# Selecting experts sequence by sequence, and modulating the token rows on GpSimd, in a two-layer adaLN kernel

## The reference

```python
h = _layernorm(x) * (1 + cb) + sb              # the modulated tokens
scores = sigmoid(h @ w_router); sfc = scores + corr_bias       # 32 columns
group_scores = sum of the 2 best sfc of each of 8 groups of 4
masked = sfc where the group is one of the 4 best, else -inf
topk_idx = top_k(masked, 6);  topk_w = scores at topk_idx
routed = sum over the 6 experts of topk_w * (silu(h @ gate_w) * (h @ up_w)) @ down_w
shared = (silu(h @ sh_gate_w) * (h @ sh_up_w)) @ sh_down_w
x = x + gb * (routed + shared)
```

## Time and profile before

| | us |
|---|---|
| median of 3 runs | 491.87 (491.0 to 492.24) |
| profiled execution | 492.93 |
| its span | 491.1 |
| PE busy | 411.1 (84%) |
| DVE busy | 310.0 (63%) |
| ACT busy | 191.6 (39%) |
| POOL busy | 130.9 (27%) |

### The profile page before, as it was taken

The page is one execution under the profiler, slowest core; times in us unless marked ns, Lnnn a source line. Parts: engine busy times, 40 slices in busy tenths (PEclk is TensorE's granted clock), DMA queues, the critical chain, the costliest instruction groups (busy, mean ns, idle before and its releaser), DMA issues. The chain is left out here.

```text
span 491.1 us, 5936 instructions
## 1 busy us (share of the span) xinstructions
PE 411.1 (84%) x1819; PEld 293.8 (60%) x1820; DVE 310.0 (63%) x726; ACT 191.6 (39%) x332; POOL 130.9 (27%) x143
## 2 busy tenths in 40 slices
PE   2888524598699999999998797389898999799995
PEld 0342123454477777777776536267676778688885
DVE  3489996879434444444443479868677956865432
ACT  2168670323222222222222144272696169422430
POOL 0160000000367777777777302000000000000000
PEclk9999775769799999999999989599999799899998
DMA  8309867395122333333337287700400000000101
GB/s 280 138 20 356 317 173 197 111 390 237 42 86 98 101 102 107 95 103 102 106 106 254 83 296 273 232 5 17 177 0 1 1 0 1 0 0 10 35 1 43
DMA packets 22878, 57.64 MB, mean 117 GB/s; under 512 B 3267, under 2 KB 14021, under 8 KB 21865
## 3 DMA queue, kind: packets, MB, share of 16 engines
q1 hardware_dynamic: 17432, 42.57, 25.4%
q0 software_dynamic: 5424, 14.82, 9.5%
HBM read 46.87 MB, written 10.51 MB: 117 GB/s over the span
## 5 line engine op out<-in xcount | busy, mean ns | idle before, releaser
L642 PE MATMUL bank<-arena,tile_mem 128*128 x224 | 76.8, 466 | 0.0
L1173 POOL DMA_INDIRECT tile_mem<-h_dram,gidx x57 | 55.4, 972 | 54.1 <-DVE gidx L1521 36.7
L1143 POOL TENSOR_TENSOR rstd<-ve,mhalf 128x4 f32<-128x4 f32 x8 | 8.1, 1015 | 212.6 <-DVE ve L1273 212.6
L1537 DVE TENSOR_TENSOR tile_mem<-tile_mem,bank 128x176 f32<-128x176 f32 x56 | 19.0, 338 | 68.7 <-ACT tile_mem L987 68.7
L1180 POOL DMA_INDIRECT y_dram<-norm,didx x56 | 55.3, 988 | 24.6 <-issue 13.4
L658 PE MATMUL bank<-arena,tile_mem 88*128 x224 | 57.7, 379 | 0.8 <-DVE tile_mem L1532 0.8
L658 PEld LDWEIGHTS bank<-arena,tile_mem 88*128 88x128 f32 x224 | 42.4, 190 | 15.8 <-issue 1.0
L738 PE MATMUL bank<-x_r,f_r 128*128 128x512 f32 x192 | 46.8, 404 | 4.3 <-DVE arena L1712 3.2
L642 PEld LDWEIGHTS bank<-arena,tile_mem 128*128 128x128 f32 x224 | 38.7, 193 | 12.1 <-issue 0.5
L738 PEld LDWEIGHTS bank<-x_r,f_r 128*128 128x128 f32 x192 | 36.6, 193 | 13.4 <-DVE arena L1712 3.7
L982 ACT ACTIVATE tile_mem<-bank 128x256 f32<-128x256 f32 x57 | 21.9, 384 | 51.4 <-PE bank L635 50.5
(11 more groups left out here) (244 smaller groups left out, 708.9 us busy)
## 6 DMA issues: line engine op xcount, KB each, us to landing
arena<-w_gu SPq DMA_DIRECT2D x3, 2112.0 KB, 14.0
arena<-y_dram SPq DMA_DIRECT2D x8, 768.0 KB, 5.8
arena<-w_dn SPq DMA_DIRECT2D x4, 1408.0 KB
arena<-w_gu SPq DMA_DIRECT2D x2, 2464.0 KB, 16.4
arena<-w_f SPq DMA_DIRECT2D x6, 512.0 KB, 7.5
arena<-w_conv SPq DMA_DIRECT2D x5, 320.0 KB, 5.8
arena<-wmod SPq DMA_DIRECT2D x3, 512.0 KB, 8.4
arena<-wmod SPq DMA_DIRECT2D x2, 768.0 KB, 6.7
```

The costliest lines, as they stand in the source:

```text
L642: mm = pe.matmul(bank[2 + r % 2][:, 0:2 * M], xgT[r % 2][:, k * P:(k + 1) * P], gu[:, bass.ds(e[k], 2 * M)], start=(k == 0), stop=(k == CT ...
L1173: pool.indirect_dma_start(out=xg[j % 4], out_offset=None, in_=h2_dram, in_offset=bass.IndirectOffsetOnAxis(ap=gidx[:, j:j + 1].bitcast(U32 ...
L1537: tt(hid[r % 2], sil[r % 2], bank[2 + r % 2][:, M:2 * M], ALU.mult).then_inc(hid_ready, 1)
```

## The change

The selection is put into a function `choose(b)` that handles the four tiles of one sequence. ScalarE takes the sigmoid of sequence 0 right after the modulation of sequence 0, and that of sequence 1 after the modulation of sequence 1; `logit_done`, `score_ready` and `mask_ready` count the sequences. TensorE waits for the scores of sequence 0 before it writes the logits of sequence 1 to the same bank. The four modulating operations move from VectorE to GpSimd (`unmix`), behind its four inverse roots. Shift and scale rows and the temporaries get other places in memory (the temporaries in the one-hot memory, in `cmp8` and in `pos`). ScalarE's wait for the modulated rows ahead of the shared expert goes.

```diff
--- before.py
+++ after.py
@@ -47,6 +47,7 @@
 SHM = 2 * M
 SHT = 3
 SH_ROWS = [P, P, SHM - 2 * P]
+TOPS = NT * (3 * G + 2 * (G + 8 - TOPG) + 8)
 SLOT_TILES = 80
 QUADS = SLOT_TILES // 4
 TAIL = 3
@@ -168,27 +169,13 @@
         hidT = [tile_mem[0:MH, o + i * 2 * P:o + (i + 1) * 2 * P] for i in range(2)]; o += 2 * C
         yt = [norm[:, TB + r, :] for r in range(4)]
         modrow0 = tile_mem[0:B, 0:6 * C]
-        modB0 = tile_mem[:, 6 * C:6 * C + B * 3 * C].rearrange("p (b n) -> p b n", b=B)
+        ga0 = tile_mem[:, 6 * C:6 * C + B * C].rearrange("p (b n) -> p b n", b=B)
+        h2_rows = tile_mem[:, (SHT + 1) * S:(SHT + 1) * S + B * 2 * C].rearrange("p (b n) -> p b n", b=B)
         sh_hid = tile_mem[:, 0:SHT * S].rearrange("p (m n) -> p m n", m=SHT)
         sh_sil = tile_mem[:, SHT * S:(SHT + 1) * S]
 
 
         scores = sb("scores", [P, NT, E])
-        o = (SHT + 1) * S
-
-        def temp(*shape):
-            nonlocal o
-            n = NT * int(np.prod(shape))
-            o += n
-            assert o <= TW
-            names = "abc"[:len(shape)]
-            return tile_mem[:, o - n:o].rearrange(f"p (t {' '.join(names)}) -> p t {' '.join(names)}",
-                                                  t=NT, **dict(zip(names, shape)))
-        sfc = temp(E)
-        hi2, lo2 = temp(G, 2), temp(G, 2)
-        m1, m2, m3 = temp(G), temp(G), temp(G)
-        gsx, gtop, grep = temp(G + 8 - TOPG), temp(8), temp(G + 8 - TOPG)
-        gmask, gpen = temp(G), temp(G)
         sfx = sb("sfx", [P, NT, E + 8 - TOPK])
         stop8 = sb("stop8", [P, NT, 8])
         srep = sb("srep", [P, NT, E + 8 - TOPK])
@@ -198,6 +185,7 @@
         ones16 = sb("ones16", [P, P], BF16)
         iota16 = sb("iota16", [P, P], F16)
         cmp8 = sb("cmp8", [P, E, G])
+        assert E * G == 2 * NT * G * 2
         ntile = sb("ntile", [P, E])
         incl = sb("incl", [P, E])
         onesE = sb("onesE", [P, E])
@@ -210,10 +198,27 @@
         wk = sb("wk", [P, NT, TOPK])
         OS = 8
         onehot_s = sb("onehot_s", [P, OS, P], F16)
+        assert 2 * TOPS <= OS * P
 
         OJ = TB * TOPK
         onehot_j = nc.alloc_sbuf_tensor_at("onehot_j", [P, OJ, SLOT_TILES + 1], F16, offset=norm_at + 4 * TB * C)
         assert OJ * (SLOT_TILES + 1) <= 2 * TB * C
+
+
+        tops_mem = onehot_s[:, :, :].rearrange("p o q -> p (o q)").bitcast(F32)[:, 0:TOPS]
+        sfc = pos[:, :, :]
+        hi2, lo2 = [cmp8[:, 16 * i:16 * (i + 1), :].rearrange("p e g -> p (e g)").rearrange("p (t g a) -> p t g a", t=NT, a=2)
+                    for i in range(2)]
+        o = 0
+
+        def temp(n):
+            nonlocal o
+            o += NT * n
+            assert o <= TOPS
+            return tops_mem[:, o - NT * n:o].rearrange("p (t a) -> p t a", t=NT)
+        m1, m2, m3 = temp(G), temp(G), temp(G)
+        gsx, gtop, grep = temp(G + 8 - TOPG), temp(8), temp(G + 8 - TOPG)
+        gmask, gpen = m1, m2
         ejcmp = sb("ejcmp", [SLOT_TILES, E])
         ej = sb("ej", [SLOT_TILES, 1])
         eoff = sb("eoff", [1, SLOT_TILES + 8], I32)
@@ -402,8 +407,8 @@
             sp_.dma_start(modg_dram, modg[0:B, :]).then_inc(mod_out[0], 16)
             sp_.wait_ge(mod_out[0], 32)
             for b in range(B):
-                for dst, row, at in ((modB0[:, b, 0:C], modg_dram, 0), (modB0[:, b, C:2 * C], mod_dram[0], SB),
-                                     (modB0[:, b, 2 * C:3 * C], modg_dram, 2), (gb0[:, b, :], modg_dram, 1)):
+                for dst, row, at in ((ga0[:, b, :], modg_dram, 0), (h2_rows[:, b, 0:C], mod_dram[0], SB),
+                                     (h2_rows[:, b, C:2 * C], modg_dram, 2), (gb0[:, b, :], modg_dram, 1)):
                     src = row[b:b + 1, at * C:(at + 1) * C].to_broadcast([P, C])
                     sp_.dma_start(dst, src).then_inc(modB_in[0], 16)
 
@@ -565,11 +570,13 @@
                 transposes(B + b, b, (x_done, b + 1))
 
                 pe.wait_ge(hT_ready, CT * (B + b + 1))
+                if b:
+                    pe.wait_ge(score_ready, b)
                 for t in range(b * TB, (b + 1) * TB):
                     for k in range(CT):
                         mm = pe.matmul(bank[6][:, t * E:(t + 1) * E], hT[:, k, t * P:(t + 1) * P], router[:, k, :],
                                        start=(k == 0), stop=(k == CT - 1))
-            mm.then_inc(logit_done, 1)
+                mm.then_inc(logit_done, 1)
 
 
             def shared_in(b, parts):
@@ -596,7 +603,7 @@
             pe.wait_ge(modcol_ready, 3)
             shared_in(0, range(3))
 
-            pe.wait_ge(mask_ready, 1)
+            pe.wait_ge(mask_ready, B)
             m16 = mask16[:, :, :].rearrange("p t e -> p (t e)")
             pe.matmul(bank[0][:, 0:NT * E], tri16[:, :], m16, start=True, stop=False, skip_group_check=True)
             for d in range(1, NT):
@@ -605,7 +612,7 @@
             for t in range(NT):
                 mm = pe.matmul(bank[1][:, 0:E], ones16[:, :], m16[:, t * E:(t + 1) * E], start=(t == 0), stop=(t == NT - 1))
             mm.then_inc(rank_done, 1)
-            pe.wait_ge(score_ready, 1)
+            pe.wait_ge(score_ready, B)
             shared_in(0, range(3, 2 * SHT))
 
             pe.wait_ge(ej_ready, 1)
@@ -942,10 +949,16 @@
                 ins = act.activation(dst[:, w * sc:w * (sc + 1)], bank[4][:, w * sc:w * (sc + 1)], ACT.Identity, bias=1.0)
             ins.then_inc(modcol_ready, 1)
             modulated(2, 0, 0, SB, CB)
+
+            def token_scores(b):
+
+                act.wait_ge(logit_done, b + 1)
+                act.activation(scores[:, b * TB:(b + 1) * TB, :].rearrange("p t e -> p (t e)"),
+                               bank[6][:, b * TB * E:(b + 1) * TB * E], ACT.Sigmoid).then_inc(score_ready, 1)
+
+            token_scores(0)
             modulated(3, 1, 0, SB, CB)
-            act.wait_ge(logit_done, 1)
-            act.activation(scores[:, :, :].rearrange("p t e -> p (t e)"), bank[6][:, 0:NT * E], ACT.Sigmoid)\
-               .then_inc(score_ready, 1)
+            token_scores(1)
 
             def shared_silu(b, extra=None):
                 for m in range(SHT):
@@ -967,7 +980,6 @@
                     ins = act.activation(dst, bank[banks[h]][:, :], ACT.Copy)
                 ins.then_inc(shy_ready, 1)
 
-            act.wait_ge(h2_ready, B)
             shared_silu(0)
 
             for t in range(NT):
@@ -1166,6 +1178,20 @@
             for n in range(B, 2 * B):
                 inverse_root(n)
 
+            def unmix(b):
+
+                pool.wait_ge(normT_done, CT * (B + b + 1))
+                pool.wait_ge(norm_ready, B + b + 1)
+                v = norm[:, b * TB:(b + 1) * TB, :]
+                sh, sc = [h2_rows[:, b, i * C:(i + 1) * C].unsqueeze(1).to_broadcast([P, TB, C]) for i in range(2)]
+                step(pool.tensor_tensor(v, v, sc, ALU.mult))
+                settle()
+                pool.tensor_tensor(v, v, sh, ALU.add).then_inc(h2_ready, 1)
+
+            pool.wait_ge(modB_in[0], 16 * 4 * B)
+            for b in range(B):
+                unmix(b)
+
             def gather(j):
 
                 if j >= 4:
@@ -1378,72 +1404,69 @@
             tmp0 = [t1[0], t2[0]]
             dve.wait_ge(yT_ready, CT * B - 1)
             dve.wait_ge(modB_in[0], 16 * 4 * B)
-            residual(X, 0, modB0[:, 0, 0:C], 1, 1, tmp0)
+            residual(X, 0, ga0[:, 0, :], 1, 1, tmp0)
             for t in range(TB):
                 norm_stats(t, X)
             outputs(3)
             layer_norm(2, X, stats_done=True)
             dve.wait_ge(yT_ready, CT * B)
-            residual(X, 1, modB0[:, 1, 0:C], 2, 2, tmp0, (2, 3))
+            residual(X, 1, ga0[:, 1, :], 2, 2, tmp0, (2, 3))
             layer_norm(3, X)
 
-            for b in range(B):
-                dve.wait_ge(normT_done, CT * (B + b + 1))
-                v = norm[:, b * TB:(b + 1) * TB, :]
-                sh, sc = [modB0[:, b, i * C:(i + 1) * C].unsqueeze(1).to_broadcast([P, TB, C]) for i in (1, 2)]
-                step(tt(v, v, sc, ALU.mult))
-                settle()
-                tt(v, v, sh, ALU.add).then_inc(h2_ready, 1)
-
+            def choose(b):
+
+                dve.wait_ge(score_ready, b + 1)
+                ts = slice(b * TB, (b + 1) * TB)
+                step(tt(sfc[:, ts, :], scores[:, ts, :], cbias[:, :].unsqueeze(1).to_broadcast([P, TB, E]), ALU.add))
+                settle()
+
+                f4 = sfc[:, ts, :].rearrange("p t (g a b) -> p (t g a) b", g=G, a=2)
+                fl = lambda v: v[:, ts].rearrange("p t g a -> p (t g a)")
+                tt(fl(hi2), f4[:, :, 0], f4[:, :, 1], ALU.max)
+                step(tt(fl(lo2), f4[:, :, 0], f4[:, :, 1], ALU.min))
+                settle()
+                tt(m1[:, ts], hi2[:, ts, :, 0], hi2[:, ts, :, 1], ALU.max)
+                tt(m2[:, ts], hi2[:, ts, :, 0], hi2[:, ts, :, 1], ALU.min)
+                step(tt(m3[:, ts], lo2[:, ts, :, 0], lo2[:, ts, :, 1], ALU.max))
+                settle()
```

(79 more changed lines are left out.)

## The result

The changed kernel took 496.02 us in the median of 8 runs, the kernel before 492.06 in 8 runs beside it: ratio 1.0088, 95% interval 1.0057 to 1.0119, so 2.8 to 5.9 us slower. Two of the eight runs before, of 497.5 and 497.7, fell in a slower state of the chip and are left out of the ratio, which makes the middle 4.3 us where the medians differ by 4.0. I had forecast 491.8. In the profiled execution the span went from 491.1 to 494.0 us.

What follows compares the result with a forecast made beforehand. Bound: a latency chain to the token indices, ahead of all expert tiles. Rank gain -0.54 plus normalization stretch +0.4 gave -0.1 us: 491.8 against a median of 491.87, range 490.6 to 497.5.

Steps and rivals of the forecast that it cites:

- Modulation off VectorE: Four 1.22 us operations leave VectorE before 1.93 us of idle time ahead of the scores; removal alone worth 0.
- Selection in halves: VectorE's expert selection, 8.2 us whole, takes 5.15 us per half, so the mask comes 3.05 us earlier.
- TensorE is late next: Three shared-expert blocks ending at 108.37 precede TensorE's rank, so it gains 0.54 us, not 3.05.
- Modulation on GpSimd: Four 128x1024 operations on GpSimd, 3.0 us each, end at 104.6 (101.8 to 107.8).
- the reading that I had put for that end: If GpSimd's 512-column operation stood still during VectorE's two-input operation, it runs 1.13 us, and 2.3 for 1024 columns.
- GpSimd beside VectorE: VectorE's normalization of sequence 1, overlapped by GpSimd's first operation, loses 0.4 us (0 to 0.52), from the row at 23.64.
- The rival of the hold: VectorE operations with two SBUF inputs stand still until GpSimd's running operation ends; middle +4.5 us, 496.4; chance 0.34.
- The clock's 2.9 us at worst: Within the hold rival, TensorE idling for the mask lowers its clock, slowing three shared blocks by up to 2.9 us.
- Stores, late loads: Later token-row store and three late expert loads stay hidden before VectorE's first comparison and TensorE's tile transpose; cost 0.

Runs made afterwards that it cites:

- e2: The changed kernel, but GpSimd modulates only one column of 256 of each token row; ratio 0.9962 to the kernel before.
- p2: The changed kernel, but GpSimd modulates partitions 0 and 1 alone; one run, 496.45 us (kernel before: 492.53).
- p3: The changed kernel, but each of GpSimd's four operations is cut into four of 256 columns; ratio 1.0074 to the kernel before.
- p1: The changed kernel, but GpSimd multiplies by 1.0 and adds 0.0 with one-input TENSOR_SCALAR operations; one run, 491.43 us (kernel before: 492.53).
- v1: The changed kernel, but VectorE modulates sequence 0 while waiting for TensorE, sequence 1 between selections, GpSimd none; ratios to kernel before 0.9996, again 0.9958.

## Why the prediction was wrong

- *Modulation off VectorE:* right. e2 shows the time up to the second sigmoid unchanged without it.
- *Selection in halves:* 5.15 us forecast, 5.45 measured (106.54 to 111.99), counted as the 8.2 were.
- *TensorE is late next:* right where GpSimd is kept out. e2 gained 0.8 us at the rank, forecast 0.54; the idle 0.59 us is gone and the shared blocks took 8.24 us, 0.07 less.
- *Modulation on GpSimd:* each 2.34 us, at the lower end (2.3) of my range and not at my 3.0. The four end at 104.32, inside my 101.8 to 107.8 (whose upper end adds up to 107.6). p2 gives 2.33 for 1024 columns beside a VectorE that stands still, which makes the reading that I had put for that end the likelier one: of the 1.64 us for 512 in the earlier trace rows some 0.5 were spent behind VectorE's two-input operation in the earlier trace rows. p3 speaks for a hold in that direction too (a piece took 0.74 us in the mean, a quarter of 2.34 is 0.59); no run had 512 columns without VectorE beside them. I had this reading in my hand and chose against it.
- *GpSimd beside VectorE:* **this step failed.** I put 0.4 us and the ends at 0 and 0.52; it was 4.03 (5.41 - 1.38), and 3.4 of these came through to the rank. The end came from one row whose GpSimd operations were TENSOR_SCALAR, and the new ones are TENSOR_TENSOR. p1 against the changed kernel is that difference, with the input that goes with it: 1.4 us against 4.0. The second GpSimd operation, too, lies beside the normalization only because the first had held that up.
- *The rival of the hold* was the true case, with 0.34 against my 0.50, and it priced +4.5 us where 4.3 was measured. Only because the stated range, 490.6 to 497.5, took in this price does 496.02 lie in it; the sum had no such loss. And the price was in part luck, since its way there was partly wrong. I let only operations with two SBUF inputs be caught, so all of its loss stood in the selection. The normalization, with one tensor input, was caught first; it alone made the shared blocks end 3.6 us late (111.66 - 92.01 against 108.37 - 92.35), and TensorE then waited only 0.37 us for the mask. The clock's 2.9 us at worst did not come either: the second shared blocks took 5.40 us as before.
- *Stores, late loads:* right, cost 0: e2 has them all and no loss.

The Trainium skill (SBUF — State Buffer, "Who interferes with whom") says that the second to issue fully blocks, and lists `tensor_scalar` among the operations that can enter a two-port mode. I had taken the normalization as outside of such a mode. The changed kernel agrees with the full block against a GpSimd TENSOR_TENSOR (2.35 us beside one of 2.34). Beside a GpSimd TENSOR_SCALAR, which reads SBUF too, p1 does not agree: behind a GpSimd operation of 2.81 us that had started before it, the first normalization took 1.06 us and the next two 0.40.

What it is in the normalization that lets it be caught stays open. It has one tensor input, but reads the mean and the inverse root of each token from SBUF as well, and no run leaves these out. L1445, which has only constants besides its tensor, was caught too.

## What to carry to other kernels

An operation moved to GpSimd is not hidden because GpSimd is idle: ask which VectorE operations run beside it, and count for each GpSimd TENSOR_TENSOR one VectorE operation that stands until it ends, on the path or not. Before a row is used as the nearest case, compare the operation and its number of tensor inputs on both engines, not only the line that is delayed. And look for idle time of the engine that already does the work: v1 needed 2.5 us of it, where the kernel before had 3.48 (and p3's profile 2.30, so it is not always there).

## What the runs showed of the hardware

- A GpSimd TENSOR_TENSOR of 1024 fp32 columns takes 2.33 to 2.40 us on 2 partitions as on 128, and stops a VectorE TENSOR_SCALAR (normalization, and one of 32 columns) or TENSOR_TENSOR until its end. MAX8 (in p3, at 97.45) and MATCH_REPLACE8 (in the changed kernel, 99.56 to 100.06) beside it kept their 0.39 us for four and 0.15 to 0.16 for one.
- A GpSimd TENSOR_SCALAR of 1024 columns takes 2.8 us, longer than the operation with two inputs, and holds single VectorE operations up by 0.6 to 0.9 us, others beside it not at all.
- The hold is per operation: between pieces of 256 columns (0.72 to 0.86 us each) VectorE gets an operation in (p3).
